# Identity multiplications behind each group of layer 1 of a graph network, on TensorE

## What is computed

```
def _gcn_conv(x, src, dst, ew, W, b, n_nodes):
    xW = x @ W
    deg = jax.ops.segment_sum(ew, dst, num_segments=n_nodes) + 1.0
    dinv = jnp.where(deg > 0, jax.lax.rsqrt(deg), 0.0)
    norm = dinv[src] * ew * dinv[dst]
    agg = jax.ops.segment_sum(norm[:, None] * xW[src], dst, num_segments=n_nodes)
    agg = agg + (dinv * dinv)[:, None] * xW
    return agg + b
...
    h1 = jax.nn.relu(_gcn_conv(x, src, dst, edge_weight, W1, b1, n))
    h2 = jax.nn.relu(_gcn_conv(h1, src, dst, edge_weight, W2, b2, n))
...
    x = x + _L0_gnn_ref(_layernorm(x, axis=-1), edge_index, edge_weight, L0_gnn_W1, L0_gnn_b1, L0_gnn_W2, L0_gnn_b2)
    x = x + _L0_ffn_ref(_layernorm(x, axis=-1)[None], L0_ffn_router_w, L0_ffn_w1, L0_ffn_b1, L0_ffn_w2, L0_ffn_b2)[0]
```

## Time and profile before

| | |
|---|---|
| median of 3 runs | 5185.78 us (5180.92 to 5188.4) |
| time of the profiled execution | 5181.53 us |
| its span in the profile | 5179.7 us |
| mean granted share of TensorE's clock | 0.854 |
| PE busy | 3805.5 us (73%) |
| POOL busy | 3002.4 us (58%) |
| DVE busy | 2293.3 us (44%) |
| ACT busy | 720.4 us (14%) |

### The profile page before, as it was taken

How to read it: one execution, slowest core, us unless ns; L and a number is a source line. 1 busy time by engine, 2 the same in 40 slices (tenths; PEclk the granted TensorE clock), 3 DMA queues, 4 the chain that set the end, 5 groups by cost and what they waited for, 6 DMA issues and landing times.

```text
span 5179.7 us, 82232 instructions
## 1 busy us (share of the span) xinstructions
PE 3805.5 (73%) x27222; PEld 3533.9 (68%) x27223; DVE 2293.3 (44%) x8827; ACT 720.4 (14%) x2277; POOL 3002.4 (58%) x3241
## 2 busy tenths in 40 slices
PE   3445655555555555555558999999999999999999
PEld 3424555455555555554547999889998899888998
DVE  6732222222222222222225556655565655556655
ACT  1020000000000000000001222222222222222222
POOL 0104666666666666666666666656665666656663
PEclk9998666766666666666668999999999999999999
DMA  3244333333333333333333333333333333333332
GB/s 95 62 145 121 99 97 98 99 97 97 98 97 98 98 97 98 97 97 100 96 95 93 96 98 96 95 94 96 98 97 94 95 96 97 97 94 96 95 97 60
DMA packets 243539, 500.39 MB, mean 97 GB/s; under 512 B 61452, under 2 KB 141655, under 8 KB 243178
## 3 DMA queue, kind: packets, MB, share of 16 engines
q0 software_dynamic: 150528, 411.24, 27.8%
q1 hardware_dynamic: 87210, 79.56, 4.8%
q10 hardware_dynamic: 5440, 5.01, 0.3%
HBM read 456.90 MB, written 38.67 MB: 96 GB/s over the span
## 4 chain that ended last, share of the span: by engine, by line
PE 36%; another core or an unknown queue 23%; DVE 23%; issue 14%; DVEq 3%; DMA 1%; SPq 1%; POOL 0%; ACT 0%; ACTq 0%; POOLq 0%
PE part L736 14%; DVE sel L1044 8%; PE psY L730 5%; PE psH L736 4%; PE psY L736 4%; PE psH L721 4%; DVE mix L1172 2%; DVE accbuf L1052 2%; DVEq L272 1%; PE psG L672 1%; DVE accbuf L986 1%; DVE nt L1126 1%; PE psT L680 1%; DVE lin L1101 1%
## 5 line engine op out<-in xcount | busy, mean ns | idle before, releaser
L461 POOL DMA_INDIRECT msg<-ytab,srcT x3136 | 2966.8, 946 | 1884.8 <-issue 962.4
L736 PE MATMUL part<-sel,msg 128*128 128x96 f32 x8384 | 1141.5, 294 | 106.9 <-issue 65.8
L736 PEld LDWEIGHTS part<-sel,msg 128*128 128x128 f32 x8384 | 1116.0, 212 | 121.9 <-issue 109.7
L730 PE MATMUL psY<-w_s,hS 128*128 128x256 f32 x3136 | 837.7, 390 | 22.9 <-ACT hS L553 9.0
L721 PEld LDWEIGHTS psH<-tokS,w_s 128*128 128x128 f32 x6272 | 811.0, 192 | 35.6
L1044 DVE TENSOR_SCALAR sel<-iota,relT,ewT 128x96 f32<-128x96 f32 x3136 | 834.1, 338 | 2.5 <-ACT accbuf L514 1.6
L721 PE MATMUL psH<-tokS,w_s 128*128 128x128 f32 x6272 | 813.5, 275 | 0.0
L1052 DVE TENSOR_TENSOR accbuf<-accbuf,part 128x192 f32 x524 | 185.5, 354 | 1199.4 <-remote 714.8
L553 ACT ACTIVATE hS<-psH,b_s 128x128 f32<-128x128 f32 x1568 | 487.6, 362 | 1444.4 <-PE psH L721 768.7
L680 PE MATMUL psT<-ident,xS 128*128 128x128 f32 x196 | 64.3, 429 | 776.0 <-issue 432.1
L730 PEld LDWEIGHTS psY<-w_s,hS 128*128 128x128 f32 x3136 | 543.0, 191 | 117.1 <-issue 61.3
(11 more groups left out here) (167 smaller groups left out, 2023.4 us busy)
## 6 DMA issues: line engine op xcount, KB each, us to landing
msg<-ytab,srcT POOLq DMA_INDIRECT x3136
msg<-in_x SPq DMA_DIRECT2D x194, 128.0 KB, 2.0
ytab<-xS SPq DMA_DIRECT2D x99, 128.0 KB, 14.3
ytab<-msg SPq DMA_DIRECT2D x98, 128.0 KB, 1.7
xS<-in_x SPq DMA_DIRECT2D x98, 128.0 KB
out<-res SPq DMA_DIRECT2D x98, 128.0 KB
w_s<-in_L_ffn_w ACTq DMA_DIRECT2D x2, 2048.0 KB
accbuf<-in_dst SPq DMA_DIRECT2D x1, 588.0 KB
```

The lines of the kernel that those rows point to most:

```text
L461: pool.indirect_dma_start(msg[:, r * GT + j, :], None, ytab[l], bass.IndirectOffsetOnAxis(ap=srcT[:, g * GT + j:g * GT + j + 1].bitcast(U3 ...
L730: mm = pe.matmul(psY[e % 2][:, 0:D], hS[:, e % 2, m, :], w2_s[:, e, m, :], start=(m == 0), stop=(m == KD - 1))
L736: m = pe.matmul(slot[:, h * W:(h + 1) * W], msg[:, tile0 + j, h * P:(h + 1) * P], sel[:, sel0 + j, :], start=(j == 0), stop=(j == GT - 1))
```

## The change

Behind each of the 392 groups of layer 1, PE multiplies the 128x128 identity by itself eight times. The product goes to the bank `psY1`, from which nothing in layer 1 reads. The group sums of layer 1 take turns over the five banks that are left. Layer 2 is as it was.

```diff
+KEEP = 8
...
-    wide = [*part, *psH, *psY]
+    wide, spare = [*part, *psH, psY[0]], psY[1]
...
+        def keep_busy():
+
+            for _ in range(KEEP):
+                pe.matmul(spare[:, 0:P], ident[:, :], ident[:, :], start=True, stop=True)
+
         for i in range(NI):
             s = Slot(i, i % 2) if i else None
             group(0, R * i)
+            keep_busy()
             group(0, R * i + 1)
             if s:
                 sums(0, s)
+            keep_busy()
             group(0, R * i + 2)
             if s:
                 turn_y2(s)
+            keep_busy()
             group(0, R * i + 3)
+            keep_busy()
```

## The result

The changed kernel takes 5234.49 us, median of 4 runs (5229.69 to 5238.99), against 5185.7 us of the kernel before on the same chip: a ratio of 1.0099 (95% interval 1.0087 to 1.0111), 49 us slower. The forecast was 5301 us, 115 us slower. The direction was right, the size more than twice too large.

A forecast was written before the change was run, and what follows sets the result against it. The prediction took POOL's gathers with one wait to bound layer 1, PE's work hidden. Later completions add 1.2 us over 97 turns, 116 us, giving 5301 us; range 4890 to 5510 us for 8 times in 10.

The forecast's parts named there:

- What bounds layer 1: Layer 1: POOL's stream, 20.0 us of gathers plus one wait for a late count, makes the 23.0 us turn.
- The sets: Layer 1 on PE: 64 added records, 134 a turn; 15.1 us of work at full clock, hidden under 20.0 us of gathers.
- The clock: Layer 1: PE's granted clock rises from 0.67 to near 1.0, with PE busy some 75% of the stretch.
- The completions: Layer 1: added records delay the count POOL awaits; a line between two working points gives 1.2 us more a turn.
- The signs named for it: Layer 1: POOL waits over 3.3 us a turn in two or more pauses; DVE idles several us before additions.
- the second point of the line: Layer 2's turn, 173 records in 24.9 us, joined with layer 1's 70 records in 23.0 us to price 134 records.
- The upper bound: Layer 1: one more wait of 3.3 us if a second is needed in each turn, 320 us and 5506 us.
- Five banks: Layer 1's group sums: no more than four groups are open, so five banks suffice for six; costs nothing.
- The cure: Rival, layer 1: filling PE's gaps ends late completions; turn 20.0 us, 291 us less, 4895 us; chance 0.27.
- the pause decides and not the count: Rival, layer 1: completions come with POOL's pause however many they are; turn stays 23.0 us, 5186 us; chance 0.15.
- The low clock: Rival, layer 1: PE keeps the half clock, its 28.8 us a turn bound; 563 us more, 5749 us; chance 0.08.

The follow-up runs named there:

- two wide multiplications: Changed kernel with two 128x512 multiplications behind each group instead of eight 128x128: 0.9981 and 0.9982 with prompt counts, 1.0051 with late ones, each against the kernel before.
- sixteen narrow ones: Changed kernel with sixteen 128x128 multiplications behind each group instead of eight: 1.0506, 1.0510 and 1.0507 against the kernel before, all with prompt counts.
- comparison 4: Chip 14, late counts: kernel before 5214.52 us; changed kernel again 1.0124, two 128x512 multiplications per group 1.0051, one tile 0.9925.
- the kernel with five banks: Changed kernel without any added multiplication, only the cut from six banks to five: 4756.1 us, 0.9998 against the kernel before, prompt counts.
- comparison 1: Chip 12, prompt counts: kernel before 4756.06 us; five banks only 0.9998, two 128x128 multiplications per group 0.9993, two 128x512 0.9981, sixteen 128x128 1.0506.
- one tile: No added multiplication; layer 1 sums only the first of four tiles, all gathers kept: 1.0001 with prompt counts, 0.9925 with late, against the kernel before.
- comparison 3: Chip 0, prompt counts: kernel before 4755.39 us; 128x128 multiplications per group, two 0.9993, sixteen 1.0510; two 128x512 0.9982; one tile 1.0001.

## Why the prediction was wrong in size

*What bounds layer 1.* Right. POOL's stream with its pauses sets the turn, in each of the six rows of the table. That the lateness is real for the engines that wait, and not a matter of the record's end, is now plain: where it is absent, the same program is 430 us faster.

*The sets.* Right. 64 records a turn and 134 in all. That their work on PE is hidden is shown for two wide multiplications, which occupy PE as long and with prompt counts cost nothing; sixteen narrow ones make PE the bound.

*The clock.* Half right. It rose from 0.67 to 0.87 and not to near 1.0, and PE is busy 84% and not 75%. The 75% would fit 15.1 us of work in a turn of 20.0 us; in the forecast's own 24.2 us that work is 62%. The measured share is higher, presumably because part of the work ran at the half clock.

*The completions.* This step failed, in the size of its term: "23.0 + (64 / 103) x 1.9 = 24.2 us, 1.2 us more". Measured were 23.46 - 22.98 = 0.48 us a turn in the comparison of the result, some 0.6 in comparison 4. The signs named for it came: two pauses and 4.0 us of them a turn, and 6.51 us of idling of DVE ahead of an addition. What was wrong is the second point of the line. I took the 24.9 us of layer 2 as what 173 records do to the counts. But PE alone needs 23.6 us for a turn of layer 2, as the kernel with five banks shows in the prompt comparison 1 (23.57 us a turn, PE busy all of it); 2128 busy of 2200 us stood in the earlier trace rows already. So 24.9 is PE's own work and 1.3 us of lateness on top, and it says nothing of a turn set by POOL's stream. In such a turn the price of more pauses is partly repaid, because each is shorter: one of 3.3 us became two of 2.0, and 4.0 - 3.3 = 0.7 us less the 0.30 us of issue is 0.4 of the 0.48 us. The upper bound, a second pause of 3.3 us, missed the same thing.

*Five banks.* Right: 0.9998 with prompt counts, and 0.9994 and 0.9999 with late ones, there together with an earlier wait of POOL.

*The rivals.* The cure did not happen: the sets filled the gaps and raised the clock, and POOL still had to stop for late counts, 4.0 us a turn in place of 3.3. With the wide ones it was 3.7 us a turn, at 1.0051. That the pause decides and not the count is half of what happens. A pause does bring the awaited count, but how many groups fit between two pauses changed with the records. The low clock did not come.

*What stays open.* Why counts come late in one comparison and not in the next, with the same kernel and once on the same chip. The profile shows no cause: the gathers are as long in both. That the gathers make the counts late is read from the traces, where counts catch up when POOL pauses; no kernel without gathers was run. Whether PE multiplies late or only its count is late is not shown either, as the end of a record is modelled. And whether it is the number of records or a mixture with their time that ends a run of gathers; against busy time and clock alone speaks one pair of kernels only.

## What to carry to other kernels

When a line is drawn between two stages of a kernel, ask first whether the same engine sets the pace at both ends; a stage whose own work fills its turn cannot price a wait in another. If a wait is split in two, time both pieces: the rhythm changes and the sum grows by less than the number. And when results and traces disagree by per cent, run the kernel before again beside them: here the unchanged kernel moved by 9% between comparisons, nine times the effect of the change. Read a granted clock together with the duration of one instruction that both traces have, as the next section shows.

## What the runs showed of the hardware

The largest thing was not the change. PE's counts come late while POOL issues indirect gathers in some comparisons (5183 to 5219 us) and within 0.14 us in others (4755 to 4760 us), and chip 5 showed both. Where they come late, the lateness grows as POOL gathers on (0.13, 11.9 and 21.0 us for groups of one run, with one tile), and the count for which POOL stops comes in its pause. In the kernels with a regular rhythm the pause was longer after a longer run: 1.5 us after 4 gathers in layer 2, and in layer 1 2.0 us after 8, 2.8 after 12, 3.3 to 3.4 after 16. With one tile it was 4.2 us after 32 on average, but 3.1 after 4, so the run's length alone does not set it.

The second thing is how to read the clock. Layer 1 with one tile of four, in the prompt comparison 3, as a stretch and two rows of its timeline; then the same product with the weights in the late comparison 4, and in the kernel before at full clock:

```profile
700.00:2400.00 1700.00, 583.38 (x1870) 431.57 (x1869) 513.40 (x1849) 67.92 (x170) 1282.94 (x1351) 1.00 0.38 111
...
1502.80 1.17 PE L737 MATMUL psH<-sel,msg 128*128 128x96 f32 x4 [3.82 <-DMA msg<-ytab,srcT]
...
1503.77 1.97 PE L673 MATMUL psG<-gw,aggS 128*128 128x256 f32 x4
...
1594.57 1.97 PE L673 MATMUL psG<-gw,aggS 128*128 128x256 f32 x4
...
2033.63 1.05 PE L672 MATMUL psG<-gw,aggS 128*128 128x256 f32 x4
```

In the prompt comparison PE is busy 34% of the stretch and stands idle for 3.82 us ahead of a group, and the column of the granted clock reads 1.00. The records themselves say otherwise. Four of them for the weights take 1.97 us, as in the late comparison, whose column reads 0.50 (1.2 GHz), while at a granted clock of 1.00 the kernel before needs 1.05 us for them. So this layer ran at the half clock, and the column is wrong there; why is not shown. The Trainium skill ("TensorE: Matmul & The Clock Gate", "Why this matters for your kernels") advises against idle gaps between bursts of matmuls because the clock falls in them; by their durations the records of the sparse kernel agree with that. Where POOL sets the turn the clock matters little: 4754.46 us here at the half clock, 4756.1 us with all products at 0.66, 4748.47 us with two wide multiplications at 1.00.
